# Routed experts on gathered 128-row blocks in place of every expert on every token

## The reference, cut to what matters

```python
logits = x @ router_w.T
probs = jax.nn.softmax(logits, axis=-1)
topk_w, topk_idx = jax.lax.top_k(probs, 2)
topk_w = topk_w / jnp.sum(topk_w, axis=-1, keepdims=True)
combine = zeros((T, 8)).at[arange(T)[:, None], topk_idx].add(topk_w)
def expert_step(acc, ws):                       # scanned over all 8 experts
    gw, uw, dw, ce = ws
    out = silu(x @ gw) * (x @ uw) @ dw
    return acc + ce[:, None] * out, None
shared = (silu(x @ s_gate_w + s_gate_b) * (x @ s_up_w + s_up_b)) @ s_down_w + s_down_b
return moe_out + shared
```

## Time and profile before

| | |
|---|---|
| median of 3 runs | 1460.88 us (1456.83 to 1460.98) |
| profiled execution, its own time | 1457.64 us |
| span of its trace | 1455.8 us |
| mean granted TensorE clock | 0.98 |
| PE, ACT, DVE, POOL busy | 94%, 56%, 63%, 53% of the span |
| DMA | 165.64 MB, mean 114 GB/s |

### The profile page before, as it was taken

One profiled execution on the slowest core, in us unless ns is written; L12 is line 12 of the kernel. 1 busy time (PEld: TensorE's weight loads), 2 busy tenths in 40 slices (PEclk: granted clock), 3 DMA queues, 4 the chain that ended last, 5 costly groups with the idle time before them and its releaser, 6 DMA issues. The chain is left out here.

```text
span 1455.8 us, 25701 instructions
## 1 busy us (share of the span) xinstructions
PE 1374.6 (94%) x8880; PEld 1231.8 (85%) x8880; DVE 917.8 (63%) x1781; ACT 822.4 (56%) x2172; POOL 764.7 (53%) x759
## 2 busy tenths in 40 slices
PE   6988799999999999999999997889999999999997
PEld 5877689998899989998899986678888888889896
DVE  5554565665656565666656664676777777776654
ACT  4543454445444554445554443367777687777773
POOL 1642243445344454435455434577669667766764
PEclk9999999999999999999999999899999999999999
DMA  5877333234331343323433423234233232342442
GB/s 171 292 265 263 82 93 99 74 83 115 111 87 48 106 123 100 89 52 102 124 87 79 118 80 130 78 122 128 81 103 118 85 118 90 107 131 85 127 132 72
DMA packets 85681, 165.64 MB, mean 114 GB/s; under 512 B 16720, under 2 KB 27664, under 8 KB 83248
## 3 DMA queue, kind: packets, MB, share of 16 engines
q1 hardware_dynamic: 85552, 163.99, 37.2%
HBM read 99.90 MB, written 22.09 MB: 84 GB/s over the span
## 5 line engine op out<-in xcount | busy, mean ns | idle before, releaser
L750 POOL TENSOR_TENSOR a_pr<-a_pr,a_ri 128x512 f32<-128x512 f32 x128 | 133.2, 1041 | 304.7 <-DVE a_ri L930 304.5
L807 ACT ACTIVATE a_pr<-a_score,a_nb 128x256 f32<-128x256 f32 x256 | 118.9, 469 | 270.2 <-DVE a_nb L922 270.2
L1277 POOL TENSOR_TENSOR l_pr<-l_pr,l_ri 128x512 f32<-128x512 f32 x128 | 133.2, 1041 | 136.5 <-DVE l_ri L1647 135.3
L1405 ACT ACTIVATE l_pr<-l_score,l_nb 128x256 f32<-128x256 f32 x256 | 119.1, 471 | 84.1 <-DVE l_nb L1618 83.4
L55 PE MATMUL a_job<-s_xs,s_wh 128*128 128x512 f32 x384 | 156.1, 407 | 5.1 <-PEq L204 5.1
L56 PE MATMUL a_job<-s_xs,s_wh 128*128 128x512 f32 x384 | 152.6, 397 | 0.0
L57 PE MATMUL a_job<-s_xs,s_wl 128*128 128x512 f32 x384 | 151.9, 396 | 0.0
L922 DVE TENSOR_REDUCE a_nb<-a_score 128x2 f32<-128x512 f32 x128 | 88.4, 691 | 89.7 <-PE a_score L993 89.4
L1618 DVE TENSOR_REDUCE l_nb<-l_score 128x2 f32<-128x512 f32 x128 | 87.4, 683 | 29.4 <-PE l_score L1743 29.1
L935 DVE TENSOR_TENSOR a_pt<-a_turn,a_pt 128x512 fp32r<-128x512 f32 x128 | 87.4, 683 | 24.4 <-ACT a_pt L815 24.4
L1767 PE MATMUL l_out<-s_wh,l_vp 128*128 128x256 f32 x512 | 93.1, 304 | 0.9 <-DVE s_wh L1622 0.9
(11 more groups left out here) (239 smaller groups left out, 4811.5 us busy)
## 6 DMA issues: line engine op xcount, KB each, us to landing
s_wl<-wgu_scratch SPq DMA_DIRECT2D x56, 512.0 KB, 4.7
a_sk<-a_rotk SPq DMA_DIRECT2D x384, 64.0 KB, 2.0
a_sq<-a_rotq SPq DMA_DIRECT2D x256, 64.0 KB, 2.0
s_xs<-xn_scratch SPq DMA_DIRECT2D x14, 1024.0 KB, 5.7
l_wd<-wd_scratch SPq DMA_DIRECT2D x56, 256.0 KB, 2.7
a_raw<-in_w SPq DMA_DIRECT2D x30, 256.0 KB, 3.0
wgu_scratch<-f_split SPq DMA_DIRECT2D x14, 512.0 KB, 4.5
f_praw<-in_moe_w SPq DMA_DIRECT2D x14, 384.0 KB, 3.5
```

The costliest lines, as they stand in the source:

```text
L750: pool.tensor_tensor(e, e, ri[:, n % 2, :].unsqueeze(2).broadcast_to([P, 2, SEQ]), ALU.mult)\
L807: i = act.activation(pr[:, n % 2, t, :], PS[n % 2][:, t * SEQ:(t + 1) * SEQ], ACT.Exp, bias=nb[:, n % 2, t:t + 1], accum_out=sm[:, n % 2, ...
L1277: pool.tensor_tensor(e, e, ri[:, n % 3, :].unsqueeze(2).broadcast_to([P, 2, SEQ]), ALU.mult)\
L1405: i = act.activation(pr[:, n % 3, t, :], PS[n % NPS][:, t * SEQ:(t + 1) * SEQ], ACT.Exp, bias=nb[:, n % 3, t:t + 1], accum_out=sm[:, n % 3 ...
```

## The change

Only the routed experts' work is replaced. The tokens are taken in two halves of 1024 (h = 0, 1). When the logits of a half are there, DVE finds each token's two experts, PE counts (job R: 16 small matmuls with a triangular and an all-ones matrix) and DVE works out for each (token, choice) pair its row in a list sorted by expert, every expert padded to a multiple of 128 rows; at most 24 blocks a half. POOL scatters the normalised rows (stored by SP to DRAM, loaded again as 128-row tiles) to those rows of `xg` with indirect DMAs: 8 tiles x 2 choices a half. A block is then turned (X: two transposes for its rows, two more to turn back the block before the last), multiplied with its own expert's gate and up weights (A: six matmuls of 352 columns), activated (ACT 176 columns, DVE twice), turned back, multiplied with the down weights (B: six of 256 columns), copied and stored to `yg`. Weights are fetched per block with the expert's number read from SBUF by SP: 704 KB and 512 KB, two buffers each. At the end POOL gathers each token's two rows (indirect, 2 per 128 tokens) and DVE adds them with their weights. The shared expert stays in 3 tiles a step. The planner's list is new:

```diff
-    UNIT, SLOT_GOAL, EARLY_GOAL = 10, 30.6, 14
+    COST = {"T": 4, ..., "L": 22, "R": 15, "G": 12, "U": 12, "D0": 6, "D1": 6, "X": 4, "A": 8, "B": 6}
+    UNIT, SLOT_GOAL, EARLY_GOAL = 10, 26, 26
+    TURN_AT = {-14: 1, -12: 2, -10: 3, 7: 4, 11: 5, 39: 6, 43: 7}
+    LOGIT_AT = {-11: 0, -8: 1, 12: 2, 44: 3}
+    ROUTE = [-8, 44]
+    SCATTER_AT = {ROUTE[h] + 6 + t: (h, t) for h in range(2) for t in range(NTH)}
+    FIRST_X = [ROUTE[h] + NTH + 7 for h in range(2)]
+    W = [x for part in ((0, None), (1, None), (None, 0), (2, None), (None, 1), (3, None))
+         for x in ([("S", part[0], k) for k in range(NSH)] if part[1] is None else [("B", part[1], j) for j in range(NBH)])]
...
+            credit = min(credit, 6.0) + (SLOT_GOAL - UNIT if n >= 0 else EARLY_GOAL) - sum(cost(j) for j in ITEMS[n])
+            while left and NOT_BEFORE.get(left[0], n) <= n and (credit >= cost(left[0]) / 2 or n == SLOTS[-1]):
...
+                    elif name == "A":
+                        wait_free(pe, turned(m))
+                        pe.wait_ge(gu_in[m % 2], 16 * (m // 2 + 1))
+                        for c in range(KC):
+                            i = product(pe, bank[:, 0:2 * I1], [th[:, slot_of(m), q, c * P:(c + 1) * P] for q in range(2)],
+                                        [wa[:, m % 2, q, c * 2 * I1:(c + 1) * 2 * I1] for q in range(2)], c == 0, c == KC - 1)
...
+                def expert_of(i):
+                    sp.wait_ge(S["routed"], W[i][1] + 1)
+                    return bass.DynSlice(sp.value_load(expert[0:1, W[i][1], W[i][2]:W[i][2] + 1], min_val=0, max_val=E - 1), 1)
+                def load_gu(i):
+                    if is_shared(i):
+                        src, to = dram["gu"][W[i][2]], wa[:, i % 2, :, 0:2 * D]
+                    else:
+                        src, to = dram["ge"][expert_of(i)].rearrange("e p q n -> p (e q) n"), wa[:, i % 2]
+                    wait_full(sp, ("U" if is_shared(i - 2) else "A", i - 2))
+                    sp.dma_start(to.bitcast(F32), src).then_inc(gu_in[i % 2], 16)
...
+                def scatter(h, t):
+                    pool.wait_ge(S["routed"], h + 1)
+                    pool.wait_ge(rows_in[t % NXR], 16 * ((NTH * h + t) // NXR + 1))
+                    for k in range(2):
+                        pool.indirect_dma_start(dram["xg"][h], bass.IndirectOffsetOnAxis(ap=slot[:, h, k, t:t + 1], axis=0),
+                                                gb[:, t % NXR, :], None).then_inc(rows_done[t % NXR], 16)
...
-                def combine(K):
-                    pool.tensor_tensor(ga[:, K % 2, :], ga[:, K % 2, :], cb[:, j % NCB, :], ALU.mult).then_inc(S["cmul"], 1)
...
+                    elif name == "X":
+                        dve.wait_ge(S["xb_hi"], TURNS[m] + 1)
+                        dve.tensor_tensor(th[:, m % 2, 1, columns(m)], bank[:, columns(m)], th[:, m % 2, 0, columns(m)], ALU.subtract)
+                    elif name == "A":
+                        dve.scalar_tensor_tensor(out=ga[:, m % 2, 0:I1], in0=gt[:, m % 2, 0:I1], scalar=1.0, in1=bank[:, 0:I1], ...)
+                        dve.tensor_tensor(h2[:, m % 2, 0:I1], ga[:, m % 2, 0:I1], bank[:, I1:2 * I1], ALU.mult)
...
+                act.wait_ge(S["tabs_in"], 32)
+                act.activation(tri[:, :, :], tri_raw.rearrange("p (k n) -> p k n", k=2), ACT.Copy)
                 job_out(("T", 0))
```

More of the change, by code:

```diff
@@ L1049, in attn_jobs @@
             jobs.append((("Q0", "Q1", None, None, None, "V")[u], b + 1))
[L1050 to L1051 removed]
+        if n in TURN_AT:
+            jobs.append(("T", TURN_AT[n]))
         if u in (3, 4) and b >= 1:
@@ L1069, in stage_layer1 @@
         if n >= -12:
-            credit += (SLOT_GOAL - UNIT if n >= 0 else EARLY_GOAL) - sum(cost(j) for j in ITEMS[n])
-            while left and (credit >= cost(left[0]) / 2 or n == SLOTS[-1]):
+            credit = min(credit, 6.0) + (SLOT_GOAL - UNIT if n >= 0 else EARLY_GOAL) - sum(cost(j) for j in ITEMS[n])
+            while left and NOT_BEFORE.get(left[0], n) <= n and (credit >= cost(left[0]) / 2 or n == SLOTS[-1]):
                 credit -= cost(left[0])
@@ L1076, in stage_layer1, with before @@
     JOB = {item: i for i, item in enumerate(ORDER)}
-    U_AT = {n: [K for K in range(L) if AT["U", K] == n] for n in SLOTS}
-    HID_AT = {n: [K for K in range(L) if AT["U", K] + 1 == n] for n in SLOTS}
-    SUM_AT = {AT["D1", MT * (s + 1) - 1] + 1: s for s in range(NSTEP)}
-    MERGE_AT = {max(n + 2, 2 * H1 * (s + 1) + 6) + 2 * i: (s, i) for n, s in SUM_AT.items() for i in range(4)}
+    def before(k):
+        return max([AT_STEP[j] for j in AT_STEP if j <= k and (k - j) % 2 == 0], default=None)
@@ new lines, in stage_layer1 @@
+    U_AT = {n: [i for i in SHARED if AT["U", i] == n] for n in SLOTS}
+    CLOSED = {i: AT["D1" if is_shared(i) else "B", i] for i in range(NW)}
+    HID_AT = {n: [i for i in SHARED if max(AT["U", i], CLOSED[before(STEP_OF[i] - 2)] if before(STEP_OF[i] - 2) is not None else -H1) + 1 == n] for n in SLOTS}
+    LAST_TILE = [max(i for i in SHARED if W[i][1] == s) for s in range(NSTEP)]
+    BLOCKS_DONE = [AT["B", BLOCKS[NBH * (h + 1) - 1]] for h in range(2)]
+    GATHER, MERGE = [], []
+    for s in range(NSTEP):
+        GATHER.append(max([BLOCKS_DONE[s // 2] + 3, FIRST_X[1] + 1 if s < 2 else 0] + [x + 6 for x in GATHER[-1:]]))
@@ new lines, in stage_layer1, with last_user, place @@
+    POW_AT, NORM_AT = {n + 1: m for n, m in STATS_AT.items()}, {n + 2: m for n, m in STATS_AT.items()}
+    assert len(GATHER_AT) == len(ADD_AT) == 2 * NSTEP and len(SUM_AT) == NSTEP and LAST_SUM <= SLOTS[-1]
+    assert AT["U", LAST_TILE[0]] < 7 and AT["U", LAST_TILE[1]] < 39
+    def last_user(i):
+        return AT["U" if is_shared(i) else "A", i]
+    GU_AFTER, D_AFTER, XB_AFTER, YB_AFTER, GU_AT, D_AT, XB_AT = ({} for _ in range(7))
+    def place(after, at, item, ready, i):
+        (after if AT[item] >= ready else at).setdefault(item if AT[item] >= ready else ready, []).append(i)
@@ L1082, in halves @@
+    ROWS_AT = {}
+    for h in range(2):
+        for t in range(NTH):
+            ROWS_AT.setdefault(ROUTE[h] + 4 if t < NXR else ROUTE[h] + 8 + t - NXR, []).append((h, t))
     def halves(n):
@@ new lines, in store_rows, with load_rows @@
+                def store_rows(m):
+                    sp.wait_ge(l1.xn_ready, m + 1)
+                    sp.dma_start(dram["rows"][m], xt[m % 2][:, :, :]).then_inc(rows_out[m % 2], 16)
+                def load_rows(h, t):
+                    for i in range(2):
+                        sp.wait_ge(rows_out[i], 32 * (h + 1))
+                    if h == 0 and t == 0:
+                        sp.wait_ge(S["xs_hi"], 1)
+                    if NTH * h + t >= NXR:
+                        sp.wait_ge(rows_done[t % NXR], 32 * ((NTH * h + t) // NXR))
+                    m, tt = divmod(NTH * h + t, TB)
+                    sp.dma_start(gb[:, t % NXR, :], dram["rows"][m][:, tt, :]).then_inc(rows_in[t % NXR], 16)
@@ L1639, in _ @@
                             k_lo(b + 1, (u - 8) // 4)
-                    s, r = divmod(n + 12, 2 * H1)
-                    if r in (1, 2, 3) and 0 <= s < NSTEP:
-                        routing(s, r - 1)
+                    for h in range(2):
+                        if n - ROUTE[h] in (1, 2, 4, 5):
+                            routing(h, (1, 2, 4, 5).index(n - ROUTE[h]))
                     for item in first:
```

679 lines of the change are left out of this document (432 added, 247 removed).

## The result

The changed kernel takes 1532.93 us (median of four runs, 1531.28 to 1534.75) against 1458.86 for the kernel before beside it (1456.15 to 1460.98): a ratio of 1.0515, 95% interval 1.0489 to 1.0541. It is **slower by 5%**, 117 us above the forecast of 1416 and far outside the range of 1386 to 1450.

A forecast was written before the change was run, and what follows sets the result against it. The prediction took PE to bound the kernel and summed -53 (steady stretch) + 12 (start) - 7 (end) + 2 (table) + 4 (`stage_first`) = -42 us against 1457.6, giving 1415.6, stated as 1416, with a range of 1386 to 1450.

The forecast's parts named there:

- each unit costs 483.6 / 3,894 = 0.124 us: Steady stretch, heads 0 to 127: PE time per planner unit (a 512-column matmul is two), with its small waits.
- the floor of 24 units: Steady stretch: every slot costs at least 24 units, 2.8 us; slots raised to it give 3,347 units, 416 us.
- I take 3%: Steady stretch: 12 us added for hand-overs between PE, DVE and ACT, with DVE at 89% and ACT at 88%.
- The rival of 460 us at a fill of 0.8: Steady stretch: DVE and ACT become the bound, 369 us of DVE at that fill; about 1445 us in all; chance 0.17.
- theory M: Experiments' theory: in each slot ACT's and DVE's steps run serially, each waiting for another engine's result; slots of some 3.7 us.
- rival T: Experiments' rival: in block slots ACT and DVE are simply full, 79% and 70%, whatever their order; b1 gains at most 8 us.
- I take 1.3 us each: POOL's 64 indirect DMAs: assumed issue cost; bursts of 5.2 us hidden by slack of about two slots in POOL's scaling.
- The rival's threshold of 3.6 us each: Indirect DMAs hold POOL, which sets the pace; slower than before from this cost on; chance 0.09.
- Light slots: 2.8 us: Slots with little PE work: least time a slot costs, 24 units, from one head's loop and ACT's further work.
- Weights: nothing: Per-block expert weight loads: hidden, 1 us to spare in the tightest places, no cost beyond the 3%.
- Start: 12 us and 2 for the table: Before head 0: 12 us more from PE's and DVE's added work, 2 us for ACT's first copy awaiting a DRAM table.
- End: 7 us less: After the last head: its turn no longer waits behind the last tiles, so that gap goes.

The follow-up runs named there:

- d4: Kernel before with only PE's list cut, four of the six 512-column matmuls of each G and U left out; 1443.3 us, steady stretch 471.0 us.
- a4: Changed kernel with small expert weight loads and one-column POOL writes in place of all indirect scatters and gathers; 1491.5 us.
- d2: Changed kernel with ACT's copy of X and DVE's subtraction on 32 columns instead of up to 512, waits and places kept; 1507.3 us.
- c2: Changed kernel with PE turning back the constant identity tile instead of a block's product h2, and PE's wait for A dropped; 1526.3 us.
- c3: Changed kernel with a fourth PSUM bank for the jobs, the two banks of the down products made one; 1530.5 us.
- b1: Changed kernel with ACT's copy of X put ahead of the slot's exponentials instead of behind them; 1531.1 us (two runs).
- c1: Changed kernel with DVE's part of a slot's second half of jobs put behind the next head's maximum; 1531.9 us.
- e1: Changed kernel with X leaving its bank by a plain DVE copy and the subtraction given to POOL, in slots 12 to 48 and from 77; 1537.0 us.
- a3: Changed kernel with the 32 indirect scatters replaced by one-column POOL writes; 1519.9 us.
- a2: Changed kernel with the 32 indirect gathers replaced by one-column POOL writes; 1515.2 us.
- b3: Changed kernel with gathers issued two a slot instead of four, sums later and SP's stores three slots later; 1522.7 us (two runs).
- a1: Changed kernel with expert weight loads cut to 64 columns of 704 and 64 of 512 from the third block on; 1541.6 us.
- b2: Changed kernel with EARLY_GOAL cut from 26 to 18, so fewer shared tiles stand in the slots before head 0; 1514.4 us (two runs).

## Why the prediction was wrong, step by step

**"So PE is the bound, and each unit costs 483.6 / 3,894 = 0.124 us": the step that failed.** 483.6 us divided by 3,894 units is an average, not a price. That PE's list came to 95% of the stretch said only that it could not be much shorter with that list; it didn't say that with a shorter list it would be. d4 measured what taking 412 units away gives: 0.031 us a unit, and in a4 the change's 767 units, with the blocks' new steps in exchange, gave 1.4 us of the 67.6 that the price and the floor of 24 units promised. Against the forecast's 430 us the stretch is 90 us longer: 38 of them are the indirect DMAs (a4), the other 52 are PE's work that bought nothing and the blocks' steps on ACT and DVE.

The wait that the prediction called in support, POOL's 135.3 us for `l_ri`, said nothing of it: DVE's and ACT's steps stand in that chain as well as PE's scores. The trace of before did hold a sign. From head 27 on the exponentials of successive heads stand 4.71, 2.75, 4.64 and 2.82 us apart, for slots of 32, 28, 32 and 28 units, that is 3.76 and 3.29 us at the bare pace. The alternation alone proves nothing, as the exponentials need not keep step with the scores: PE's own scores stand 3.70 to 3.76 us apart there. But two slots take 7.46 us where PE needs 7.05, and the 0.30 us that PE idles in them it waits for DVE. In a stretch's sum this does not show.

The Trainium skill ("Perfetto Trace Analysis", Identifying the Most-Contended Engine) warns that the busy share of matmuls is a poor measure of how close TensorE is to its limit, and wants the share of peak arithmetic and the busy share of the weight loads instead. Here the latter would have misled as well: it was 87% before, the highest of any engine but the matmuls themselves, and d4 shows how little stood behind it.

**DVE and ACT "hand over to each other several times a slot ... I take 3%".** The mechanism was named and mis-sized. The work came out as forecast (DVE 352.5 us, ACT 359.6 over the stretch, for 369 and 366), yet the block slots lasted 3.7 to 3.8 us where the rule with its 3% gives 3.4, 31.5 us in all over heads 11 to 55 and 76 to 117. The rival of 460 us at a fill of 0.8 had the right engines; the fill reached in block slots is 0.76 and 0.78 on ACT, 0.73 and 0.67 on DVE (the two windows above). In the kernel before it was 0.75 and 0.72, so it hardly moved, while the forecast needed 0.88. What the runs show is a limit on ACT and DVE that moves when work goes (d2), and not when one dependency (c2), a bank (c3) or one order (b1, c1, e1) goes. The slot laid out above shows the two engines in fixed order, each waiting for the other's result of the same slot. How much of the limit is this order (theory M) and how much the plain sum of their work (rival T) is not shown: T foresaw b1 and e1, M foresaw d4, and d2 fell between them. Which rearrangement would open it stays open; none of four did.

**Indirect DMAs: "I take 1.3 us each: bursts of 5.2 us are hidden by that slack".** The price was right: a median of 0.97 us and a gap of 0.30. The hiding was wrong, and not by POOL's scaling alone, as the rival had it. Scatters hold `pow_x` of sequence 4, and so the norm, its transposes (PE waited 6.0 us) and the first X (3.5 us for its load): a3 gives 17 us for heads 7 to 11 and 55 to 57. Gathers make DVE and SP wait in order: a2 gives 20 us for heads 66 to 76 and 117 to 127. The rival's threshold of 3.6 us each asked for POOL's total, but place in the lists counted too: b3 got 10.2 us back with every issue kept. The wait for `l_xb` was foreseen at 3 us in each half; PE had one of 3.47 us in the first half and none in the second.

**Light slots: 2.8 us.** Right at full clock, but the price left out that PE's clock falls in such slots: 3.84 us then, at a granted clock of 0.67 from 1470 to 1503.6 us, with waits of PE up to 4.29 us. The Trainium skill ("TensorE: Matmul & The Clock Gate", Part 1) has it that the array's clock is 1.2 GHz when it is idle and 2.4 GHz when it is busy; the trace agrees. So the work left to PE ran slower in these slots, where it had little else to do.

**Weights: nothing.** Right (a1), at a DMA share of 0.59 to 0.60 for the blocks' slots, 0.6 to 0.7 forecast.

**Start: 12 us and 2 for the table.** Mis-sized: head 0 lies 37.2 us later, 6.0 of them before `stage_layer1` begins to depend on the change (4 were forecast for it), 31 in the start itself. b2 shows the larger part: moving shared tiles out of slots -12 to -1, where PE's granted clock was 0.76, takes 21 us off the time to head 0, of which less than 3 are lost again behind it. The table held ACT until 920.4 us, so that its first copy of turned rows came 4.5 us after PE's first transposes where it had been 1.1 before: 3.4 us for the 2 forecast. The rest, some 6 us, no run divides.

**End: 7 us less.** Wrong: 25.9 us from head 127, before 25.7. The gathers, sums and merges of the last step stand where the last tiles stood.

The three misses, 19 us at the start, 90 in the steady stretch and 7 at the end, make 116; the profiled execution (1531.28 us) lies 115.7 above the sum's 1415.6.

## What to carry to other kernels

An engine that is busy for 95% of a stretch need not be what paces it: set the spacing of one recurring instruction of its own against its load, over one period of the pattern, and see what ends its small waits; where a second limit lies right below, its work has no price until a run with that work cut gives one. A restructuring that trades PE's work for small dependent steps on ACT and DVE is paid for in the loop maximum, exponentials, copies, products, next maximum; write down that loop for a slot of each kind, and count what stands in it. For a burst of DMA issues, list on every in-order queue what is behind the issue, behind the landing and behind the store; for the gathers those waits cost more here than the issues.

## What the runs showed of the hardware

DVE's sum of a gathered row tile (L1832: 256 columns, two inputs in SBUF) takes 0.47 to 0.55 us when POOL works on no tensor beside it, as in 16 of the 32, and 1.0 to 2.5 us in the 12 that lie for 0.9 us or more beside one of POOL's elementwise operations. At 1269.58 us two of them took 2.41 us while POOL multiplied and added at full width; POOL's two took 1.26 and 1.32 us, little more or less than elsewhere. The Trainium skill ("GPSIMD Engine Reference", section 8) has it that POOL shares its SBUF interfaces with DVE and contends with DVE instructions that have two inputs in SBUF; the trace agrees. The 32 sums took 30.0 us, for 13.2 in the prediction, which had put this inside its 3%.

```profile
1269.04 1.26 POOL L1465 TENSOR_TENSOR l_y<-l_y,l_s 128x512 f32<-128x512 f32 x1
1270.38 1.32 POOL L1467 TENSOR_TENSOR s_x<-s_x,l_y 128x512 f32<-128x512 f32 x1
```

In a1 a 64 KB load of 256-byte pieces landed in 2.2 us (median), a 704 KB one in 5.7, so an eleventh of the bytes took well over a third of the time.
